# Issuing the stores of the attention probabilities from ScalarE's queue instead of SyncE's

## What is computed

```python
xn = layernorm(x)
# attention, H = 16 heads of 8 features, with relative positions clipped to +-20
q, k, v = proj(Wq, bq), proj(Wk, bk), proj(Wv, bv)        # of xn
idx = clip(pos[None, :] - pos[:, None], -20, 20) + 20
attn = softmax((einsum('bhqd,bhkd->bhqk', q, k) + einsum('bhqd,qkd->bhqk', q, rel_k[idx])) / sqrt(8))
w1 = einsum('bhqk,bhkd->bhqd', attn, v)
w2 = einsum('bhqk,qkd->bhqd', attn, rel_v[idx])
a = (w1 + w2).reshape(B, S, E) @ Wo.T + bo
# the second part, on xn: attention over 4 heads with one shared key and value, then a mixture of 8 experts, top 2
out = x + a + ffn(xn)
```

## Time and profile before

| what | us |
|---|---|
| median of 3 runs | 2386.11 |
| lowest, highest run | 2382.93, 2386.49 |
| the profiled execution, its own time | 2381.51 |
| its span, first to last instruction | 2379.7 |
| first exponential of row 0 | 92.70 |
| first exponential of row 9, of row 10 | 872.45, 958.87 |
| `attend` hands over to `mix` | about 1489 |

### The profile page before, as it was taken

The page is one execution under the profiler, slowest core; times in us unless marked ns, Lnnn a source line. Parts: engine busy times, 40 slices in busy tenths (PEclk is TensorE's granted clock), DMA queues, the critical chain, the costliest instruction groups (busy, mean ns, idle before and its releaser), DMA issues. The chain is left out here.

```text
span 2379.7 us, 77272 instructions
## 1 busy us (share of the span) xinstructions
PE 2097.2 (88%) x27816; PEld 1436.8 (60%) x27816; DVE 1854.2 (78%) x4151; ACT 1591.6 (67%) x4178; POOL 1030.8 (43%) x1270
## 2 busy tenths in 40 slices
PE   3498898889888899889898887699999969999999
PEld 1366666666666666666666665366666636665665
DVE  1388889889988988988988986477676647777777
ACT  2387888888888888888888875477777642232222
POOL 3346656656665665665666553010010013333331
PEclk7699999999999999999999998699999979999999
DMA  3355655656665665665665543000100020100100
GB/s 115 97 126 136 158 141 136 155 150 134 149 151 143 137 151 137 140 159 135 135 159 145 119 107 60 27 28 27 35 31 26 26 72 27 31 26 26 38 28 18
DMA packets 571232, 228.63 MB, mean 96 GB/s; under 512 B 465590, under 2 KB 543030, under 8 KB 566326
## 3 DMA queue, kind: packets, MB, share of 16 engines
q1 hardware_dynamic: 514102, 190.53, 33.7%
q10 hardware_dynamic: 56832, 34.09, 4.8%
HBM read 129.61 MB, written 94.90 MB: 94 GB/s over the span
## 5 line engine op out<-in xcount | busy, mean ns | idle before, releaser
L834 ACT ACTIVATE a_probs<-a_bank_s,a_neg_max 128x512 f32<-128x512 f32 x1024 | 698.2, 694 | 140.2 <-DVE a_neg_max L666 138.2
L666 DVE TENSOR_REDUCE a_neg_max<-a_bank_s 128x2 f32<-128x1024 f32 x512 | 627.0, 1225 | 55.3 <-ACT a_probs L834 0.9
L467 PE MATMUL a_bank_pt<-a_ident,a_probs 128*128 128x128 f32 x4096 | 589.1, 283 | 69.5 <-ACT a_feat_t L849 38.8
L467 PEld LDWEIGHTS a_bank_pt<-a_ident,a_probs 128*128 128x128 f32 x4096 | 439.4, 142 | 204.7 <-issue 93.3
L808 ACT ACTIVATE a_probs_t<-a_bank_pt 128x512 f32<-128x512 f32 x512 | 311.6, 609 | 95.8 <-PE a_bank_pt L467 77.8
L648 DVE COPY a_probs_t<-a_bank_pt 128x512 f32<-128x512 f32 x512 | 350.3, 684 | 17.1 <-PE a_bank_pt L467 7.2
L489 PE MATMUL a_bank_o<-a_probs_t,a_v 128*32 128x128 f32 x8192 | 277.9, 276 | 1.7 <-DVE a_probs_t L648 0.3
L1557 ACT ACTIVATE e_gate<-e_bank_g 128x512 f32<-128x512 f32 x144 | 85.9, 597 | 274.9 <-PE e_bank_g L1496 274.9
L489 PEld LDWEIGHTS a_bank_o<-a_probs_t,a_v 128*32 128x32 f32 x8192 | 209.7, 110 | 55.3 <-issue 50.5
L631 DVE TENSOR_TENSOR a_bank_s<-a_bank_s,a_win 128x144 f32<-128x144 f32 (+2 forms) x640 | 161.2, 271 | 99.0 <-PE a_bank_s L455 95.8
L956 POOL TENSOR_TENSOR a_win<-a_raw,a_band 128x1152 f32<-128x1152 f32 x64 | 168.7, 2637 | 159.8 <-issue 81.4
(11 more groups left out here) (167 smaller groups left out, 3552.2 us busy)
## 6 DMA issues: line engine op xcount, KB each, us to landing
scr_probs<-a_probs SPq DMA_DIRECT2D x512, 72.0 KB, 3.0
a_raw<-scr_qr SPq DMA_DIRECT2D x256, 96.0 KB
scr_qr<-a_qr ACTq DMA_DIRECT2D x64, 320.0 KB, 4.1
a_feat<-scr_probs SPq DMA_DIRECT2D x256, 78.0 KB, 2.6
a_left<-scr_probs SPq DMA_DIRECT2D x256, 64.0 KB, 2.4
scr_parts<-a_sp ACTq DMA_DIRECT2D x96, 128.0 KB
scr_parts<-a_sp SPq DMA_DIRECT2D x48, 128.0 KB
a_q<-scr_parts SPq DMA_DIRECT2D x32, 192.0 KB
```

What stands on the lines that cost most here:

```text
L467: ins = nc.tensor.transpose(b_pt[bank_of(job)][:, 0, t * P:(t + 1) * P], probs[(u - 1) % 4][:, j, MAX_REL + t * P:MAX_REL + (t + 1) * P], ...
L666: nc.vector.tensor_reduce(neg_max[:, 2 * pair:2 * pair + 2], b_s[:, 2 * pair:2 * pair + 2, :], AX.X, ALU.max, negate=True).then_inc(max_ok, 1)
L834: nc.scalar.activation(probs[u % 4][:, j, MAX_REL:MAX_REL + S], b_s[:, j, :], ACT.Exp, bias=neg_max[:, j:j + 1], accum_out=sums[:, t, PLAC ...
```

## The change

The two stores of a unit are no longer issued by SP at the end of its unit. ScalarE issues them one unit later: in unit u, behind the second L808 (pair 1) and ahead of the two exponentials of pair 1, it waits for the exponentials of unit u-1 and issues that unit's two stores. For units 4t it first waits for the read back of two tiles ago, as SP did. The stores of unit 15 are issued in unit 0 of the next row, those of the last row in the shortened row. SP's wait for landed stores ahead of L305 stays. Line numbers: L834 becomes L839, L849 becomes L854, L376 becomes L749; PE's and DVE's lines go down by 15.

```diff
--- before.py
+++ after.py
@@ -363,21 +363,6 @@
                     if not first and u == 11:
                         sp.wait_ge(y_ok, b * 2 + 2)
                         sp.dma_start(scr["y"][b - 1], y_in[:]).then_inc(y_st, 16)
-                    if tail:
-                        continue
-                    if u % 4 == 0:
-                        need(sp, f_in, b, 64 * NT, 64 * (t - 1))
-                        need(sp, l_in, b, 64 * NT, 64 * (t - 1))
-                        sp.sem_inc(room, 1)
-                    sp.wait_ge(exp_ok, b * 4 * UNITS + 4 * u + 4)
-                    for i in (0, 2):
-                        at = PROBS_AT[t % 2] + (i * H + head_of(u, i) * NJ) * QBLK * WIN
-                        own = probs[u % 4][:, PLACES.index(i), t * P + i * QBLK:]
-                        sp.dma_start(bass.AP(scr["probs"].tensor, at, [[WIN, P], [H * QBLK * WIN, 2], [1, WIN]]),
-                                     bass.AP(own.tensor, own.offset,
-                                             [own.ap[0], [2 * (S + 2 * MAX_REL) + QBLK, 2], [1, WIN]])
-                                     ).then_inc(p_out[u % 4], 16)
-
             for sm, start in ((y_st, 16), (y_ok, 2)):
                 sp.sem_inc(sm, start)
             for u in range(UNITS):
@@ -750,6 +735,21 @@
             def middle(n, k):
                 act.wait_ge(rest_ok[k], n + 1)
                 nc.scalar.activation(SP[k][1][:], rest[k][:], ACT.Copy).then_inc(mid_ok[k], 1)
+
+            def store(b, u):
+
+                t = u // 4
+                if u % 4 == 0:
+                    need(act, f_in, b, 64 * NT, 64 * (t - 1))
+                    need(act, l_in, b, 64 * NT, 64 * (t - 1))
+                act.wait_ge(exp_ok, b * 4 * UNITS + 4 * u + 4)
+                for i in (0, 2):
+                    at = PROBS_AT[t % 2] + (i * H + head_of(u, i) * NJ) * QBLK * WIN
+                    own = probs[u % 4][:, PLACES.index(i), t * P + i * QBLK:]
+                    act.dma_start(bass.AP(scr["probs"].tensor, at, [[WIN, P], [H * QBLK * WIN, 2], [1, WIN]]),
+                                 bass.AP(own.tensor, own.offset,
+                                         [own.ap[0], [2 * (S + 2 * MAX_REL) + QBLK, 2], [1, WIN]])
+                                 ).then_inc(p_out[u % 4], 16)
 
             def prep(b, u):
                 n = b + LEAD
@@ -820,6 +820,11 @@
                     for pair in range(2):
                         if (u and not tail) or (u == 0 and not first):
                             read_probs(b, u, 2 * pair)
+                        if pair and u:
+                            if not tail:
+                                store(b, u - 1)
+                        elif pair and not first:
+                            store(b - 1, UNITS - 1)
                         if tail:
                             continue
                         act.wait_ge(max_ok, b * 2 * UNITS + 2 * u + pair + 1)
```

## The result

The changed kernel takes 2454.5 us (2449.6 to 2457.4), the kernel before in the same comparison 2385.3 us; the ratio is 1.029 with an interval of 1.028 to 1.031. That is 69 us slower. Slower was forecast, but at 2410, with a range up to 2440: the direction was right, the size almost three times too small.

A forecast was written before the change was run, and what follows sets the result against it. VectorE was taken to set most of the pace, TensorE and ScalarE the rest. 8.3 + 6.0 + 4.9 + 3 + 1.9 = 24 us on the median of 2386.1 gave 2410 (2396 to 2424 if its mechanism holds), range 2387 to 2440.

The forecast's parts named there:

- The price of an issue: A store's issue costs the same on either queue, 0.469 us in the median on SP; an undisturbed pair takes 0.88.
- the hold of 1.0 to 1.1 us: In open units, two stores put the exponential of pair 1 about 1.08 us behind the second L808, making it 0.55 late.
- Removed from SP: SP loses 15 us of issue per row of 86; costed at zero, since no wait that matters ends earlier.
- the faster rival: SP's queue was the hidden cause of lateness, so VectorE's waits for scores shrink: 2378 us, chance 0.07.
- Place A: Unit 15 to 0: late exponentials pass on to VectorE's copy; slip 0.55 us, times 15 row ends, 8.3 us.
- Place B: Units 3 to 5: late exponentials delay TensorE and VectorE's copy; slip 0.4 us, times 15 rows, 6.0 us.
- Place C: Units 11 to 13: the same chain one tile on; slip 0.35 us, times 14 rows, 4.9 us.
- Two kinds alternate: Per row, nine covered units cost 0; in seven open ones the exponentials are 0.55 us late, repeating from row to row.
- Cost 0: Unit 1, a covered pair: stores end at 880.4, before VectorE's maxima allow the exponential at 880.96, so no loss.
- long issues: Stores on ScalarE's queue: 2 in 224 applied to 512 gives 5 long issues at 0.6 us each, 3 us.
- long issues follow the stores: Rival: long issues belong to this transfer or a busy SP, adding 18 to 37 us; 2425 to 2444, chance 0.13.
- The end: After the last row: the last stores are issued later, L305 starts later and the serial work behind adds 1.9 us.

The follow-up runs named there:

- s3: Against the change, only stores issued in units 1, 2, 4, 6, 7, 8, 10, 12, 14 stay on ScalarE, the others return to SP: 2404.3 us.
- s4: Against the change, only stores issued in units 0, 3, 5, 9, 11, 13, 15 stay on ScalarE, the others return to SP: 2423.8 us.
- s2: Against the change, both stores stay on ScalarE but move ahead of the second half's copy of the scores (second L808): 2394.6 us.

## Why the prediction was right or wrong

- *What bounds the kernel* stands but for the clock, below. VectorE sets the pace, and the change costs where VectorE becomes idle. Its wait for scores is 3.9 us in the undisturbed row after, and new waits for the transposes came with it. That L305 would start 3 to 7 us earlier did not come: by the first exponential of the unit it starts 0.5 later in unit 5, 0.7 later in unit 9 and 2.2 earlier in unit 13 (medians of rows 1 to 13). GpSimd's wait for the read back fell from 15.0 to 13.0 and nothing followed, as forecast:

```profile
POOL a_left L941 <- DMA a_left<-scr_probs: 13.0, 2, 6.6
...
DVE a_bank_s L616 <- PE a_bank_s L440: 3.9, 6, 1.0
```

- *The price of an issue* stands (0.437 against 0.469, a pair 0.89), and so does *the hold of 1.0 to 1.1 us* in open units.
- *Removed from SP, at zero* stands. Nothing gets faster by it in any run; the faster rival is out.
- *Place A* stands: 0.53 in unit 15, 15 times, is 8.0 us for 8.3.
- **Place B failed in size.** Forecast 0.4 a row; units 3 and 5 together are 0.74 longer, 11 us. **Place C failed in size**: 0.35 forecast, 1.0 measured in units 11 and 12, 14 us. The step that failed is "Two kinds alternate": each unit was judged by the trace of before, as if the units ahead of it would stay on time. A held unit makes TensorE late, so that the next unit's copy has no dispatched work ahead of it, and a covered unit becomes open (4 and 12). Holds don't just add, they take away each other's cover: units 1, 5 and 12 in s3, s4 and the change show it. Unit 7, in none of the places, is 0.21 longer, 3 us.
- **Unit 1 failed**: "Cost 0". By the earlier trace rows its stores were to be over 0.56 before the exponential. With unit 0 on time that holds (s3: the stores begin 0.69 behind the unit's first exponential and the unit costs 0.04); in the change unit 0 is held too, and they begin 1.28 behind it. Four issues of L724 stand behind the exponential of pair 1 and already held ScalarE; any lateness passes straight through them:

```profile
378.90 0.69 ACT L839 ACTIVATE a_probs<-a_bank_s,a_neg_max 128x512 f32<-128x512 f32 x1 [0.36 <-DVE a_neg_max L651]
379.06 0.72 ACTq L724 DMA_DIRECT2D scr_qr<-a_qr_first  x1
...
380.51 1.38 ACTq L724 DMA_DIRECT2D scr_qr<-a_qr_first  x2
381.99 0.60 ACT L808 ACTIVATE a_probs_t<-a_bank_pt 128x512 f32<-128x512 f32 x1 [1.64 <-issue]
```

  The unit is 0.58 longer in the median, nearly 9 us in 15 rows. Here the idle time ahead of the exponential is 0.36 instead of 0.21.
- **The term "long issues" failed most in proportion**: five at 0.6 us, 3 us, against 28 long issues and 24 us of scattered loss, of which some 11 are left without the clock's own part. "I take this end because rows of ScalarE's own queue are the nearest" chose rows that were too few. The rival *long issues follow the stores* had the kind of loss right, with a chance of 0.13. That 24 us lies in its 18 to 37 is in part luck, since half of it is the clock; and its total of 2425 to 2444 was still short, because it stood on my steady part.
- **"A clock of 1.00, so the clock is no part of this" failed**: it was read from one row of before, and the price of a TensorE that waits longer was put at nothing. Measured: a lower clock in six of rows 1 to 13 instead of one, some 13 us.
- *The end*: the last read back (L305) starts 4.1 us behind the end of the last exponential instead of 2.6, so 1.5 us, and `mix` 1.4 later, for the 1.9 forecast.

Steady 48 us (forecast 19), scattered 24 (3 and nothing for the clock), the end 1.4 (1.9): the steady part is the larger share of the error. One sum was also off on its own terms: a third less to half more of 24 us is 2402 to 2422, not 2396 to 2424.

## What to carry to other kernels

In this kernel a DMA issue on a compute engine's queue is free while the instructions dispatched ahead of it last, and nearly all loss beyond that; count the whole batch of issues between two pieces of compute against that cover, not the new ones alone, and put them behind the longest piece that has just been released by its wait. Before moving issues, try them one at a time: here one at the bad place cost 3.5 us, two 69, and two at a good place 11. A unit that is covered in the trace of before is covered only as long as the unit ahead of it stays on time. And look at the granted clock of every row, not of one: where TensorE waits longer, its clock may fall, which cost about 1.5 us a time here.

## What the runs showed of the hardware

- An issue's time hardly depends on its size: 0.414 us for 16 rows of 64 bytes, 0.437 for 72 KB in rows of 288 bytes, both in pairs; 0.377 for the large one alone.
- ScalarE's queue runs several instructions ahead of the engine: in s2 the issues begin 0.09 after the first of two exponentials has started, with the second already dispatched. It doesn't run past an issue: in the rows shown above the compute behind starts some 0.1 to 0.2 us after the issues end. The Trainium skill (Advanced Engine Details and Errata, Sequencer Loop) says that engine instructions are pushed into a queue, and that others can be read and queued while a control instruction executes. The first half agrees; if a DMA issue is taken for such a control instruction, the second doesn't, by the 0.52 of "issue" at 1001.50.
- About 4 in 100 stores issued by ScalarE in the change took 1.0 to 2.2 us, and one in 256 when ScalarE issued one at a time beside SP. Of the 28 long issues 18 overlapped one of SP's and 10 did not, so a wait for the other queue alone doesn't explain them. Their cause stays open.
- Behind a TensorE wait of 2.34 us the granted clock was at the lower level (1.2 GHz), and eight transposes took 1.95 instead of 1.09 us. Nine such stretches reach into rows 1 to 14 of the change, each begun in a wait of 1.52 to 2.83 us or just after it, against one before.
